# Four fused layers on one core: item maxima and a block's projections moved, and the mixer's x convolution written as shifted matmuls

## What is computed

```python
x = x + _L0_attn_ref(_layernorm(x), ...)   # mixer
x = x + _L0_ffn_ref(_layernorm(x), ...)    # attention and experts
x = x + _L1_attn_ref(_layernorm(x), ...)   # selective scan
x = x + _L1_ffn_ref(_layernorm(x), ...)    # gated network of four linear stages
```

```python
zxbcdt = u @ W_in.T
dt = jax.nn.softplus(zxbcdt[..., -NHEADS:] + dt_bias)
xBC_c = conv_general_dilated(xBC_c, conv_w, padding=[(D_CONV - 1, 0)], feature_group_count=D_XBC)
xBC = _silu(jnp.transpose(xBC_c, (0, 2, 1)) + conv_b)
h = exp(dt_t * A) * h + dt_t * x_t * B_t       # per head, state of 16
y_t = einsum(h, C_t) + D_param * x_t
y = layernorm(y); y = sigmoid(y @ W_gate.T + b_gate) * y
return concatenate([_silu(z0) * x0, y]) @ W_out.T
```

## Time and profile before

| | us |
|---|---|
| median of three executions | 1397.04 |
| lowest, highest | 1392.69, 1397.04 |
| profiled execution, its own time | 1396.32 |
| its span | 1394.6 |

### The profile page before, as it was taken

How to read it: one execution, slowest core, us unless ns; L and a number is a source line. 1 busy time by engine, 2 the same in 40 slices (tenths; PEclk the granted TensorE clock), 3 DMA queues, 4 the chain that set the end, 5 groups by cost and what they waited for, 6 DMA issues and landing times.

```text
span 1394.6 us, 15919 instructions
## 1 busy us (share of the span) xinstructions
PE 1176.6 (84%) x5728; PEld 592.8 (43%) x5728; DVE 914.9 (66%) x1716; ACT 788.5 (57%) x1139; POOL 290.2 (21%) x204
## 2 busy tenths in 40 slices
PE   3666676788998999999999999999967759689998
PEld 1444343343433333333333365656523324237776
DVE  5677863688788788887854363444377786883443
ACT  4667843244544565555678754545767665525554
POOL 2233344200000000000001110010086766860000
PEclk9678888699999999999999999999989988899999
DMA  2122167324300000000000121211031312100000
GB/s 80 57 61 62 46 108 116 68 45 90 46 1 1 1 1 1 1 1 1 1 17 17 61 66 46 95 49 38 24 137 68 107 68 77 68 30 0 8 8 16
DMA packets 51966, 62.43 MB, mean 45 GB/s; under 512 B 7848, under 2 KB 42288, under 8 KB 49840
## 3 DMA queue, kind: packets, MB, share of 16 engines
q1 hardware_dynamic: 51888, 61.43, 17.2%
HBM read 50.53 MB, written 4.46 MB: 39 GB/s over the span
## 4 chain that ended last, share of the span: by engine, by line
PE 54%; DVE 21%; ACT 10%; POOL 7%; issue 6%; DMA 1%; SPq 0%; DVEq 0%; POOLq 0%; ACTq 0%
DVE mx L1086 8%; PE psum L1172 8%; PE psum L1459 7%; PE psum L1144 6%; PE psum L1074 6%; PE psum L382 5%; PE psum L384 5%; PE psum L383 5%; POOL drive L1899 4%; PE psum L1850 3%; DVE hst L1917 2%; ACT probs L1158 2%; DVE cacc L642 1%; ACT psum L1859 1%; ACT edec L595 1%
## 5 line engine op out<-in xcount | busy, mean ns | idle before, releaser
L1158 ACT ACTIVATE probs<-psum 128x1024 f32<-128x1024 f32 (+1 forms) x320 | 288.7, 938 | 206.9 <-PE psum L1144 106.4
L1086 DVE TENSOR_REDUCE mx<-psum 128x1 f32<-128x512 f32 (+3 forms) x640 | 345.8, 601 | 68.6 <-PE psum L1074 51.3
L1074 PE MATMUL psum<-kz,qa 128*128 128x512 bf16 (+3 forms) x640 | 196.1, 359 | 30.9 <-DVE mx L1086 20.4
L1144 PE MATMUL psum<-qa,kz 128*128 128x512 bf16 (+1 forms) x640 | 184.7, 363 | 7.5 <-ACT probs L1158 4.3
L1850 PE MATMUL psum<-hst,ident 128*128 128x512 f32 x256 | 132.8, 664 | 41.3 <-DVE hst L1917 22.2
L1899 POOL TENSOR_TENSOR drive<-du,b_bc 128x1024 f32<-128x1024 f32 x64 | 149.5, 2358 | 21.7 <-DVE hst L1917 21.1
L1477 DVE TENSOR_TENSOR hid<-hid,gate_bc 128x1024 f32<-128x1024 f32 x64 | 78.8, 1241 | 109.0 <-ACT hid L1469 106.9
L1172 PE MATMUL psum<-probs,v 128*32 128x512 f32 (+3 forms) x1280 | 149.9, 541 | 0.1
L1917 DVE TENSOR_TENSOR_SCAN hst<-psum,hlast,drive 128x512 f32<-128x512 f32 x96 | 115.7, 1264 | 31.7 <-ACT psum L1859 26.2
L1469 ACT ACTIVATE hid<-psum,cols 128x512 f32<-128x512 f32 x128 | 85.0, 689 | 75.6 <-PE psum L384 75.1
L1074 PEld LDWEIGHTS psum<-kz,qa 128*128 128x128 bf16 x640 | 61.5, 99 | 135.3 <-DVE mx L1086 84.8
(11 more groups left out here) (286 smaller groups left out, 1824.3 us busy)
## 6 DMA issues: line engine op xcount, KB each, us to landing
b_bc<-b_rows SPq DMA_DIRECT2D x16, 1024.0 KB, 4.7
cs_bc<-cs_rows SPq DMA_DIRECT2D x16, 512.0 KB, 6.4
gate_bc<-gate_rows SPq DMA_DIRECT2D x32, 256.0 KB, 3.2
ew_raw<-experts_dram SPq DMA_DIRECT2D x8, 512.0 KB, 3.7
qk_part_rows<-qk_parts SPq DMA_DIRECT2D x8, 384.0 KB, 2.8
qa<-qk_part_rows SPq DMA_DIRECT2D x48, 64.0 KB
...
```

Of the source, the lines that this page charges most:

```text
L1074: ins = pe.matmul(out[:, 0:w], qa[:, b, h // 2, i * P:(i + 1) * P], kz[:, h // 8, c, h % 8, 0:w], start=True, stop=not last, skip_group_ch ...
L1086: dve.tensor_reduce(mx[:, 4 * i + h % 4, c:c + 1], fill_bank("mx", k, n)[:, 0:w], AX.X, ALU.max).then_inc(S["mx_read"], 1)
L1144: ins = pe.matmul(out[:, lo:], kz[:, h // 8, kt // TPB, h % 8, kt % TPB * P:(kt % TPB + 1) * P], qa[:, b, h // 2, lo:], start=True, stop=n ...
L1158: act.activation(probs[:, st % 2, hh, :, lo:], s_pair[n % 2][:, :, lo:], ACT.Exp, scale=SCALE).then_inc(S["p_done"], 1)
```

## The change

It has three parts.

1. **x convolution as matmuls.** Four weight tiles `wk[:, k, :]` are formed once by POOL, the x columns of the input projection times tap k. In front part 3 XA and XB are each one accumulation of four matmuls over `x0T`, which now keeps three columns of history, shifted by k (L450 after). ACT applies the silu straight from PSUM. DVE's convolution keeps B and C alone. The projections go in the order B, C (part 1), dt, z, x0 (part 2), XA, XB (part 3). A table of taps, 1024 numbers, is loaded and spread over the partitions.
2. **First maxima inside the end steps.** The maxima of item 0 are put into steps 16, 17 and 19, those of item 1 into 20 and 21, in the banks 3, 4 and 7 that the chunks no longer use. Their mrow transfers move up in SP's list.
3. **Block 3's prep in attention.** Part 1 (xn, inner) goes after item 0's first step on DVE and its second on PE and ACT; part 2 (q, k, v) into item 1's first step, part 3 into item 1's second. The four PSUM results go through `ring_m`.

```diff
+PJ_ORDER = (BREP, CREP, DTREP, Z0A, Z0B, X0A, X0B, XA, XB)
+PJ_ACT = (BREP, CREP, DTREP, Z0A, Z0B)
...
-        cacc = sb("cacc", [P, 4, BLK], F32)
+        cacc = sb("cacc", [P, 2, BLK], F32)
+        wk = sb("wk", [P, CONV, DI], F32)
...
-            return {("front", 0): [("x", b, 0)], ("front", 1): [("pj", b, j) for j in range(4)],
-                    ("front", 2): [("pj", b, j) for j in range(4, 9)],
+            return {("front", 0): [("x", b, 0)], ("front", 1): [("pj", b, j) for j in PJ_ORDER[0:2]],
+                    ("front", 2): [("pj", b, j) for j in PJ_ORDER[2:7]], ("front", 3): [("pj", b, j) for j in PJ_ORDER[7:9]],
...
+            if part == 3:
+                if b == 0:
+                    pe.wait_ge(S["wk_ready"], CONV)
+                for j in PJ_ORDER[7:9]:
+                    out = ring.take(pe, "pj", b, j)
+                    for k in range(CONV):
+                        ins = pe.matmul(out[:, :], wk[:, k, j * P:(j + 1) * P], x0T[:, k:k + BLK], start=(k == 0), stop=(k == CONV - 1))
+                    ins.then_inc(S["pj_filled"], 1)
...
-                for n, j in enumerate(CONV_ORDER):
-                    act.wait_ge(S["conv_done"], 4 * b + n + 1)
-                    act.activation(xs[b % 2][:, j, :], cacc[:, j, :], ACT.Silu, bias=C("conv0_b", j)).then_inc(S["xs_ready"], 1)
+                for n, j in enumerate((BREP, CREP)):
+                    act.wait_ge(S["conv_done"], 2 * b + n + 1)
+                    act.activation(xs[b % 2][:, j, :], cacc[:, n, :], ACT.Silu, bias=C("conv0_b", j)).then_inc(S["xs_ready"], 1)
+                for j in (XA, XB):
+                    act.activation(xs[b % 2][:, j, :], pj(j), ACT.Silu, bias=C("conv0_b", j)).then_inc(S["xs_ready"], 1)
...
             load_k_sp(sp, 1)
+            mrow_sp(sp, 0)
             store_sp(sp, 2)
+            mrow_sp(sp, 1)
 
             sp.wait_ge(S["x_mixed"], NB)
-            mrow_sp(sp, 0)
-            mrow_sp(sp, 1)
...
+        PREP_PE = {(0, 1): 1, (1, 0): 2}
+        PREP_ACT = {(0, 1): 1, (1, 0): 2, (1, 1): 3}
+        PREP_DVE = {(0, 0): 1, (1, 0): 2}
...
+        EARLY_PE = {16: [("mx", 0, n) for n in range(3)], 17: [("mx", 0, n) for n in range(3, 9)],
+                    19: [("mx", 0, n) for n in range(9, 16)], 20: [("mrow", 0)] + [("mx", 1, n) for n in range(4)],
+                    21: [("mx", 1, n) for n in range(4, 16)] + [("mrow", 1)]}
+        EARLY_DVE = {17: EARLY_PE[16] + EARLY_PE[17], 19: EARLY_PE[19], 20: EARLY_PE[20], 21: EARLY_PE[21]}
...
+            if name in early.at:
+                if early.at[name] == 0:
+                    pe.wait_ge(S["y_done"], G)
+                return early.take(pe, *name)
...
+            sp.dma_start(tap_bc[:, :, :].rearrange("p k m -> p (k m)"), a["taps"].partition_broadcast(P)).then_inc(S["in_taps"], 16)
...
+            front_pool(o, pool, 0, 0)
+            pool.wait_ge(S["in_win"], 16)
+            pool.wait_ge(S["in_taps"], 16)
+            for k in range(CONV):
+                pool.tensor_tensor(wk[:, k, :], w_raw[:, 0:DI], tap_bc[:, k, :], ALU.mult).then_inc(S["wk_ready"], 1)
...
             prep_dve(o, dve, NB - 1, 0)
-            first_maxima_dve(o, dve, 0)
-            prep_dve(o, dve, NB - 1, 1)
-            first_maxima_dve(o, dve, 1)
-            prep_dve(o, dve, NB - 1, 2)
-            dve.wait_ge(S["bo_added"], NB)
             attention_dve(o, dve)
...
             pe.wait_ge(S["v_done"], NB - 1)
-            first_maxima_pe(pe, 0)
-            prep_pe(pe, NB - 1, 1)
-            first_maxima_pe(pe, 1)
-            prep_pe(pe, NB - 1, 2)
-            pe.wait_ge(S["qk_evac"], 2 * NB)
-            pe.wait_ge(S["v_done"], NB)
+            pe.wait_ge(S["mrow_done"], 4)
             attention_pe(pe)
```

110 lines of the change are left out of this document (69 added, 41 removed).

## The result

The changed kernel took 1388.94 us as the median of its five runs, the kernel before 1397.04 in the same comparison (five runs, 1392.69 to 1397.32): the medians lie 8.1 us apart. One of the five runs was in a slow state (1951.45 us at a mean granted clock of 0.556): it counts in that median and in nothing else here, and the other four lie from 1379.35 to 1390.94 us with a median of 1386.88. The ratio without it is 0.9922, 95% interval [0.9902, 0.9942], or 10.9 us. Forecast was 1374.4 with a range up to 1388. The sign was right and the gain at most half of what the sum gave. The profiled execution took 1388.94 us (span 1387.2, mean granted clock 0.946; before 1396.32, 1394.6 and 0.932).

A forecast was written before the change was run, and what follows sets the result against it. No engine is full in the mixer, which waits in turn for each engine's queue; later work follows in rigid order. 1396.3 - 1.6 - 1.0 - 8.0 - 13.9 + 2.6 = 1374.4 us, range 1366 to 1388.

The forecast's parts named there:

- T1: Block 0's front: z's first projection is filled earlier, so ACT's chain starts earlier; new POOL products hidden; -1.6 us.
- T2: Block 1, step 1: PE's convolution-side work halves, so chunk 2 waits for DVE's mdec instead; -1.0 us.
- Rival 4: Mixer fronts: the 16 long PE records of three fronts fall wholly on the path, slower, 1407.5 us; chance 0.04.
- T3: Block 3 of the mixer: fewer waits on DVE and PE at full clock end it earlier; -8.0 us.
- (d): Block 3: PE's transposes no longer wait for DVE's xn but for POOL alone, 163.0 against 168.5; -5.5 us.
- rival 3: Step 11: the SBUF lock between DVE and POOL costs 1.5 to 2 us, 1376 us; chance 0.08.
- (e): Block 3's end: PE at 2.4 GHz shortens 4.8 us to 2.7 and 4.6 to 3.75; ends 8.0 us earlier.
- T4: The head: early maxima start attention 13.9 us earlier, with block 0's k loads taken as landed at 212.
- Rival 5: Head: k loads land only near 241.7, PE stands 20.5 us in step 16, no change, 1395 us; chance 0.03.
- T5: Block 3's prep inside attention items 0 and 1 adds +1.0 and +1.6 us; +2.6 us, bounds 0 and 12.9.
- Rival 2: Items 0 and 1: block 3's prep comes out in full, +10.3 us over the 2.6, 1384.7 us; chance 0.14.
- Rival 1: Block 3: ACT's table loads or POOL bound it as in block 2, gain only 0.4, 1382.0 us; chance 0.17.

The follow-up runs named there:

- e4: Changed kernel, but GpSimd starts the products of taps and weights and the memsets only after block 0's normed x is written; 1382.95 us.
- e5: The changed kernel run again unaltered, nine runs; median 1391.46 us.
- e8: Changed kernel plus 59 matmuls whose results nobody reads, ahead of seven TensorE stalls in the mixer; 1382.41 us.
- e1: Kernel before with part 1 alone (x convolution as matmuls); 1394.43 us.
- e6: Changed kernel, but SyncE sends block 1's blank rows only after block 0's loads have landed; 1385.61 us.
- e7: Changed kernel with the edits of e4 and e6, and item 0's last seven maxima moved from step 19 to 18; 1387.25 us.
- e3: Changed kernel with part 3 undone: block 3's norm, q, k and v stand before the first score again; 1394.02 us.
- e10: Kernel before with part 1 alone plus the 59 idle matmuls of e8; 1385.48 us.
- e11: Changed kernel with the edits of e4, e6 and e8 together; 1370.57 us.
- e9: Kernel before plus 110 idle matmuls ahead of six TensorE stalls in the mixer; 1393.85 us.
- e16: The kernel of e11 run again; 1373.39 us.
- e13: Changed kernel with part 3 undone, as in e3, plus the 59 idle matmuls of e8; 1386.88 us.
- e2: Kernel before with parts 2 and 3 alone, convolution as before; 1388.96 us.

## Why the prediction was right and wrong

**T1 (-1.6): wrong by 3.6, the step "Hidden".** The order's gain is real: e4 shows 1.8. But the new `wk` products and the two memsets now lie beside block 0's normed x, and VectorE stood for them: +2.0. The rule of the Trainium skill that I weighed at step 11 (SBUF — State Buffer, section "SBUF: two separate sides") bears on this place just as well. The rows agree that VectorE stands, 1.1 us alone and 5.65 beside GpSimd, but not on how long: the lock is said to be held for an instruction, and the last op stood through the end of a product and two whole memsets. I had asked only when PE needs `wk`, not who works beside the products.

**T2 (-1.0): right.** From chunk 0 to chunk 4 (dt_tok) the changed kernel took 38.6 us, the kernel before 40.0: 1.4 us, of which 0.8 lie between chunks 1 and 2, where the term put its 1.0.

**Added PE work (0): right.** The idle time at the three boundaries shrank to 5.6, 2.2 and 2.9 us and never to nothing; two of the waits name POOL and the last xn. Rival 4 falls with it: no kernel with part 1 was slower than the kernel before. Block 2 (-0.4): right in this profile, 42.6 us from chunk 4's to chunk 8's dt_tok after 43.0. But e5, the same kernel, took 45.0 and e8 41.1: the clock moved this block by more than the term, and the sum had nothing for it.

**T3 (-8.0): the waits right, the clock wrong.** (a) held: no wait on x_tok, and from chunk 8's to chunk 10's dt_tok 19.2 us where the kernel before took 20.95 (forecast 18.7). (b) and (c): dt at 152.60 and silu at 159.33, 2.7 and 2.6 us earlier than in the earlier trace rows (forecast 3.55 and 3.5). (d): the transposes at 164.03 wait for xn, which met POOL's decay products and ended 0.6 us after them; so the lock cost some 0.6 us there (rival 3), and not 0.

The failing step is (e), "I take it at 2.4 GHz", and "steps 13 to 16 move by the same amount". From chunk 8's dt_tok to the last stmp the kernel before took 86.4 us; the kernels with part 1 took 79.0 (changed), 81.4 (e5), 80.6 (e1), 84.6 (e4, e6, e7) and 84.9 (e3), so the term is 1.5 to 7.4 us, by the execution. With idle matmuls they took 76.9 to 77.5 (eight traces; 77.0 in e8, e10 and e11), but the kernel before then takes 80.6 as well (e9): at a held clock the term is 3.6 us. The remaining 5.8 of the 9.4 us between 86.4 and 77.0 are the clock's, and the kernel before can have them too. The sum took 3.0 us of clock as certain in (e) (4.8 to 2.7, and 4.6 to 3.75); the other 5.0 stand against the 3.6. It was not one number, and the range did not hold it.

**T4 (-13.9): wrong by 2.6, the step "I take 212".** From last stmp to first score: 61.3 us before, 50.0 changed, so 11.3. The k loads landed at 216.5, 12.5 us behind the last issue, and not 3. The blank rows of block 1 were in the queues with them (DMA share of that stretch above 0.8), and they are part of the cause: held back, they leave 6.3 to 10.4 us of the 12.5 (six traces; e3, with the old order, has 7.8). Why even those are more than 3 stays open. Rival 5 had the place right, with 7.1 us for its 20.5. The gate matmuls at full clock gave 2.5 us back, and VectorE's meeting with y2 (3.14 for 1.1 us) took 2. In e11, with the blank rows later, the same stretch is 47.4 us, the 13.9 in full; in e16, the same kernel, it is 49.6, and 11.7 are left.

**T5 (+2.6): right, a little small.** First score to item 2's first score: 25.5 us before, 28.5 after, +3.0; up to item 2's o copy it is +4.0 (54.4 and 58.4 us, the latter in four traces). Rival 2 (+10.3) falls. Its bound of 12.9 us is itself mis-added: the terms it names come to 11.8. e13 and e3 show that the same work in front of the first score costs 3.5 to 7.7 us more in the traces.

**After item 2 (none expected): wrong in this profile, open as to the change.** 8 us were lost there: 1.0 up to item 2's o copy (T5), 1.6 in item 4 and 5.4 in the last stage. Item 4 took 29.0 us instead of 27.4 (o copy to o copy); from 330 to 345 us, behind a stall in its tail, the granted clock was 0.89, and 1.00 in the kernel before and in e4. Of the 18 traces 5 have that 1.6 us, all of kernels with early maxima (the changed kernel in both of its traces), and nine other traces of such kernels do not. Item 8 has the same step (40.5 or 39.0 us), and there the kernel before has the 40.5.

From the scan's first drive product to the end the kernel before took 377.3 us and the changed one 382.7. Of the 18 traces 14 lie from 377.0 to 378.2 and 4 from 380.5 to 382.7: the changed kernel twice (382.7 and 380.6), e2 and e7. The stage's instructions are the same in all of them. What differs is the clock from 70 to 105 us behind the first drive, 0.82 in those four and 0.95 or 0.96 in all of the others. The changed kernel and, below it, the kernel before:
```profile
1074.50:1109.50 35.00, 31.73 (x72) 14.55 (x73) 23.44 (x23) 18.50 (x26) 21.73 (x11) 0.82 0.26 86
1087.30:1122.30 35.00, 31.77 (x83) 14.49 (x81) 24.74 (x24) 23.67 (x31) 22.72 (x11) 0.96 0.23 76
```
So the loss goes with a lower clock; the first trace of the changed kernel has 2 us more of it than the other three, from 210 us on (0.88 in the next 35 us, 0.97 in e5). Whether the change brings them on is open: all four traces are of kernels with early maxima, but ten other traces of such kernels, with e4 and e8 among them, do not have them.

**The rivals.** Rival 1 left 0.4 us of term 3, and e3, e4, e6 and e7 come near it with 1.5 to 1.8. Its cause is not theirs: ACT and POOL do the same work in e8, where the stretch takes 77.0 us. The sum missed by taking each stretch's clock as settled, and no rival had that.
